# Key ring of five chunks, overlapping head groups, and row maxima turned by VectorE instead of TensorE

## The reference, cut to what matters

```
mod = (silu(c) @ wmod)                     # six vectors of 128
h = layernorm(x) * (1 + ca) + sa
q, k, v = h @ Wq + bq, h @ Wk + bk, h @ Wv + bv      # 16, 4 and 4 heads of 64
q, k = rotary(q), rotary(k)
logits = q . k / 8, masked causally;  w = softmax(logits);  out = (w . v) @ Wo + bo
x = x + ga * out
h = layernorm(x) * (1 + cb) + sb
x = x + gb * sum over the two best experts of weight * ((silu(h @ w1) * (h @ w3)) @ w2)
```

## Time and profile before

| | us |
|---|---|
| median of three runs | 1372.88 (1371.19 to 1373.23) |
| profiled execution, its own time | 1371.72 |
| its span, first to last instruction | 1369.8 |
| TensorE busy in the span | 1288.1 (94%) |
| VectorE busy | 916.7 (67%) |
| ScalarE busy | 566.6 (41%) |
| GpSimd busy | 551.8 (40%) |

### The profile page before, as it was taken

One profiled execution on the slowest core, in us unless ns is written; L12 is line 12 of the kernel. 1 busy time (PEld: TensorE's weight loads), 2 busy tenths in 40 slices (PEclk: granted clock), 3 DMA queues, 4 the chain that ended last, 5 costly groups with the idle time before them and its releaser, 6 DMA issues.

```text
span 1369.8 us, 18475 instructions
## 1 busy us (share of the span) xinstructions
PE 1288.1 (94%) x6732; PEld 808.2 (59%) x6732; DVE 916.7 (67%) x1775; ACT 566.6 (41%) x1178; POOL 551.8 (40%) x599
## 2 busy tenths in 40 slices
PE   2689999998999999899999999999995899999998
PEld 2445555455555555555555555555543688888887
DVE  3767877858687786868777687877648544444443
ACT  1444544554554355444444545444443222232222
POOL 2553446563354564446456344654422111110110
PEclk9799999999999999999999999999997899999999
DMA  5000000000000000000000000000001000000001
GB/s 134 1 0 1 1 1 1 1 1 1 1 1 1 1 1 1 1 1 1 1 1 1 1 1 0 1 1 0 1 1 47 0 24 23 23 23 23 23 1 31
DMA packets 18445, 12.94 MB, mean 9 GB/s; under 512 B 7104, under 2 KB 15680, under 8 KB 18368
## 3 DMA queue, kind: packets, MB, share of 16 engines
q1 hardware_dynamic: 11072, 9.58, 2.3%
q10 hardware_dynamic: 7296, 2.36, 0.7%
HBM read 10.88 MB, written 1.05 MB: 9 GB/s over the span
## 4 chain that ended last, share of the span: by engine, by line
PE 78%; DVE 14%; POOL 3%; issue 2%; ACT 1%; ACTq 1%; DVEq 0%; POOLq 0%
PE PS L1003 17%; PE PS L1051 13%; PE PS L957 10%; PE PS L985 10%; PE PS L1065 8%; PE PS L987 8%; DVE part_max L743 2%; PE PS L1013 2%; PE PS L934 2%; DVE full L759 2%; PE PS L1022 2%; PE PS L970 2%; PE PS L941 2%; DVE full L788 2%; DVE k_split L732 1%
## 5 line engine op out<-in xcount | busy, mean ns | idle before, releaser
L743 DVE TENSOR_REDUCE part_max<-PS 128x1 f32<-128x512 f32 (+2 forms) x576 | 348.0, 620 | 119.9 <-PE PS L957 94.5
L580 ACT ACTIVATE full<-PS 128x512 f32<-128x512 f32 x384 | 224.3, 598 | 230.0 <-PE PS L987 213.8
L957 PE MATMUL PS<-KT,QT 128*128 128x512 f32 (+3 forms) x640 | 262.8, 423 | 12.5 <-ACT QMT L562 5.0
L985 PE MATMUL PS<-QT,KT 128*128 128x512 f32 (+3 forms) x640 | 265.7, 415 | 1.0 <-ACT diag L589 1.0
L449 POOL TENSOR_TENSOR full<-full 128x512 f32<-128x512 f32 x128 | 165.6, 1320 | 176.8 <-PE PS L1003 175.7
L987 PE MATMUL PS<-QMT,KT 128*128 128x512 f32 (+3 forms) x640 | 233.7, 365 | 0.0
L957 PEld LDWEIGHTS PS<-KT,QT 128*128 128x128 f32 x640 | 120.7, 191 | 157.1 <-DVE part_max L743 86.9
L1003 PE MATMUL PS<-full,V 128*64 128x512 f32 x768 | 207.1, 618 | 0.0
L589 ACT ACTIVATE diag<-PS 128x512 f32<-128x512 f32 (+3 forms) x256 | 111.4, 438 | 227.8 <-PE PS L990 202.4
L853 DVE TENSOR_TENSOR full<-full,PS 128x512 f32<-128x512 f32 x128 | 88.0, 688 | 145.5 <-ACT full L629 145.5
L985 PEld LDWEIGHTS PS<-QT,KT 128*128 128x128 f32 x640 | 122.8, 192 | 90.8 <-ACT diag L589 32.1
(11 more groups left out here) (109 smaller groups left out, 1628.7 us busy)
## 6 DMA issues: line engine op xcount, KB each, us to landing
full<-in_L_ffn_experts_w_dram SPq DMA_DIRECT2D x24, 256.0 KB, 2.9
out_dram<-XA SPq DMA_DIRECT2D x4, 256.0 KB, 2.3
wqkv<-in_L_attn_Wq_dram ACTq DMA_DIRECT2D x1, 512.0 KB, 4.3
bqkv<-in_L_attn_bq_dram ACTq DMA_DIRECT2D x1, 512.0 KB, 10.1
wo_sb<-in_L_attn_Wo_dram SPq DMA_DIRECT2D x1, 512.0 KB, 8.7
sin_sb<-in_k_sin_dram ACTq DMA_DIRECT2D x1, 512.0 KB, 8.2
full<-in_L_wmod_dram SPq DMA_DIRECT2D x1, 384.0 KB, 9.5
cos_sb<-in_k_cos_dram ACTq DMA_DIRECT2D x1, 256.0 KB, 9.5
```

The costliest lines, as they stand in the source:

```text
L580: nc.scalar.activation(full[:, k % QUADS, r, :], PS[:, bank, :], ACT.Exp).then_inc(probs_ready, 1)
L743: nc.vector.reduce_max(part_max[:, t, b:b + 1], PS[:, bank, 0:width], AX.X).then_inc(ring_dve, 1)
L957: last = nc.tensor.matmul(PS[:, bank, 0:w], QT[:, ch % 2, h, t * P:(t + 1) * P], KT[:, 0, b * BANK:b * BANK + w], start=True, stop=not las ...
L985: nc.tensor.matmul(o, KT[:, 0, kt * P:(kt + 1) * P], QT[:, ch % 2, h, q0:BANK], start=True, stop=False)
```

## The change

`q_max` is gone. The negated maxima go to a small tile `neg_max` (128 queries x 4 heads x 4 tiles). In `maxed`, VectorE now issues four 32x32-block transposes, one for each 32 partitions, each reading one column for every tile broadcast 32 times and writing 32 partitions x 128 elements of a new tile `max_rows`; partition 64 of it is then the row of 512 maxima. Before them VectorE waits until ScalarE has copied the previous pair-step's row of the same m (`max_placed`). In `qmax`, TensorE and the ring have no part: ScalarE waits for the transposes and copies one row of 512 elements into row 64 of QMT. The 64 feature rows of QMT are written at `qk`, by one more ScalarE copy of 64 x 512 from the ring bank that holds the turned queries; ScalarE's copy into `q_max` at `low` is gone. QMT has two buffers, by chunk. TensorE waits at `s` for `max_placed` in place of the ring.

KT grows from four chunks to five (`KEY_SLOTS`), addressed as a ring over all groups' chunks by `key_at`, so the next group's first chunk has a place of its own. The groups' lists are merged by position, so that a group's last steps (its tail up to 9.3) lie between the first steps of the next. The placements of the next group's first steps and of the first maxima change.

```diff
@@ the order
-    begin.append(begin[-1] + 30.0)
+    begin += [begin[-1] + x for x in begin[1:3]]
-        place(maxima(2, 0), 0.05, 0.99),
-        place([("qmax", 2, 0)] + maxima(2, 1), 1.01, 1.74),
+        place(maxima(2, 0), 0.5, 1.25),
+        place([("qmax", 2, 0)] + maxima(2, 1), 1.27, 1.8),
-        place(parts(CHUNKS), 6.19, 7.16), place(turned(CHUNKS), 7.32, 7.47), place(max_steps(end), 7.4, 7.71),
-        place(parts(CHUNKS + 1), 7.42, 8.14), place(maxima(end + 1, 0) + maxima(end + 1, 1), 7.77, 7.85),
-        place([("qmax", end, 1)], 7.71, 7.79),
-        place(turned(CHUNKS + 1), 8.0, 8.36), place([("qmax", end + 1, m) for m in range(2)], 8.4, 8.7),
+        place(parts(CHUNKS), 5.1, 6.0), place(turned(CHUNKS), 6.1, 6.3), place(parts(CHUNKS + 1), 7.0, 7.8),
+        place(maxima(end, 0) + maxima(end, 1), 6.85, 7.4), place(maxima(end + 1, 0) + maxima(end + 1, 1), 7.4, 7.9),
+        place([("qmax", end, m) for m in range(2)], 7.9, 7.97),
+        place([("qmax", end + 1, m) for m in range(2)], 8.02, 8.3),
+        place(turned(CHUNKS + 1), 8.05, 8.5),
+        place(diag_steps(7), 8.03, 8.4), place(tail_steps(7), 8.45, 9.3),
+    steps += merge(*placed)
@@ tiles
-        q_max = sb("q_max", [P, 2, TB, QH, P], F32R)
+        neg_max = sb("neg_max", [P, QH, TB])
+        max_rows = sb("max_rows", [P, 2, BANK])
-        QMT = sb("QMT", [P, QH, BANK], F32R)
-        KT = sb("KT", [P, 2, T], F32R)
+        QMT = sb("QMT", [P, 2, QH, BANK], F32R)
+        KT = sb("KT", [P, 2, KEY_SLOTS * BANK], F32R)
+        def key_at(tile):
+            return tile // TB % KEY_SLOTS * BANK + tile % TB * P
@@ GpSimd
-            nc.gpsimd.memset(q_max[:, :, :, :, HEAD + 1:P].bitcast(F32), 0.0)
+            nc.gpsimd.memset(QMT[:].bitcast(F32), 0.0)
@@ ScalarE
-                nc.scalar.copy(q_max[:, ch % 2, b, :, 0:HEAD], q).then_inc(q_max_ready, 1)
+                        slot = n.slot_at[("q",) + x[1:]]
+                        act.wait_ge(ring_filled, slot + 1)
+                        src = PS[0:HEAD, RING + slot % RING_BANKS, :].rearrange("p (a b) -> p a b", a=QH)
+                        nc.scalar.activation(QMT[0:HEAD, ch % 2, :, t * P:(t + 1) * P], src, ACT.Copy)
-                        ring_to(QMT[:, 2 * (x[1] % PAIRS) + x[2], :], x, BANK)
+                        _, J, m = x
+                        act.wait_ge(max_ready, n.at["maxed", J, m] + 1)
+                        if J >= 2 * PAIRS:
+                            act.wait_ge(scores_ready, n.at["s", J - 2 * PAIRS, local(J - 2 * PAIRS), TB - 1, m] + 1)
+                        nc.scalar.copy(QMT[HEAD:HEAD + 1, J // PAIRS % 2, 2 * (J % PAIRS) + m, :],
+                                       max_rows[HEAD:HEAD + 1, m, :]).then_inc(max_placed, 1)
@@ VectorE, maxed
-                    dve.sem_inc(max_ready, 1)
+                    if J >= 1:
+                        dve.wait_ge(max_placed, n.at["qmax", J - 1, m] + 1)
+                    for a in range(P // 32):
+                        rows = slice(32 * a, 32 * (a + 1))
+                        to = max_rows[HEAD:HEAD + 32, m, :].rearrange("p (t q) -> p t q", q=P)[:, :, rows]
+                        last = nc.vector.transpose(to, neg_max[rows, 2 * (J % PAIRS) + m, :].unsqueeze(2)
+                                                   .broadcast_to([32, TB, 32]))
+                    last.then_inc(max_ready, 1)
@@ TensorE
-                elif kind == "qmax":
-                    _, J, m = x
-                    need(max_ready, n.at["maxed", J, m] + 1)
-                    bank = ring_bank(x)
-                    for t in range(TB):
-                        last = nc.tensor.transpose(PS[:, bank, t * P:(t + 1) * P],
-                                                   q_max[:, J // PAIRS % 2, t, 2 * (J % PAIRS) + m, :].bitcast(F32),
-                                                   ident[:])
-                    last.then_inc(ring_filled, 1)
-                    taken(("qmax", J, m))
+                    need(max_placed, n.at["qmax", J, m] + 1)
```

More of the change, by code:

```diff
@@ L166, in block_kernel @@
     next_group = [
-        place(parts(CHUNKS), 6.19, 7.16), place(turned(CHUNKS), 7.32, 7.47), place(max_steps(end), 7.4, 7.71),
-        place(parts(CHUNKS + 1), 7.42, 8.14), place(maxima(end + 1, 0) + maxima(end + 1, 1), 7.77, 7.85),
-        place([("qmax", end, 1)], 7.71, 7.79),
-        place(turned(CHUNKS + 1), 8.0, 8.36), place([("qmax", end + 1, m) for m in range(2)], 8.4, 8.7),
+        place(parts(CHUNKS), 5.1, 6.0), place(turned(CHUNKS), 6.1, 6.3), place(parts(CHUNKS + 1), 7.0, 7.8),
[4 more added lines that the diff above has]
+        place(diag_steps(7), 8.03, 8.4), place(tail_steps(7), 8.45, 9.3),
     ]
+    last_pair = [place(diag_steps(7), 8.01, 8.38), place(tail_steps(7), 8.4, 9.0)]
     def group_order(*more):
-        return merge([(float(b), x) for b, x in zip(before, main)], [(begin[end], x) for x in pending],
-                               *side, *more)
+        return [y for items in ([(float(b), x) for b, x in zip(before, main)], [(begin[end], x) for x in pending],
+                                *side, *more) for y in items]
     def of_group(order, g):
@@ L191, in block_kernel @@
             maxima_first = maxima_first[n:]
-    last_tail = place(tail_steps(-1), 0.02, 1.1)
     steps = of_group(lead_in, -1)
+    placed = []
     for g in range(GROUPS):
-        steps += of_group(group_order(*([last_tail] if g else []),
-                                      *(next_group if g < GROUPS - 1 else [place(tail_steps(end - 1), 8.4, 8.9)])), g)
+        order = group_order(*(next_group if g < GROUPS - 1 else last_pair))
+        at = [(p + g * begin[end], x) for (p, _), x in zip(order, of_group([x for _, x in order], g))]
+        placed.append(at)
+    steps += merge(*placed)
     class Counts:
@@ L213, in __init__ @@
                     "proj": [(x, "dve")], "qk": [(("q",) + x[1:], "act"), (("k",) + x[1:], "act")],
-                    "max": [(x, "dve")], "qmax": [(x, "act")], "rowsum": [(x, "dve")],
+                    "max": [(x, "dve")], "rowsum": [(x, "dve")],
                     "out": [(x, "dve")],
@@ L739, in step @@
                     if ch == 0:
[L740 removed]
+                        nc.vector.tensor_reduce(neg_max[:, 2 * (J % PAIRS) + m, t:t + 1],
                                                 PS[:, bank, 0:width], AX.X, ALU.max, negate=True).then_inc(ring_dve, 1)
@@ L956, in step @@
                     w = (t + 1) * P if last_bank else BANK
+                    keys = key_at(J // N_J * TILES + b * TB)
                     last = nc.tensor.matmul(PS[:, bank, 0:w], QT[:, ch % 2, h, t * P:(t + 1) * P],
-                                            KT[:, 0, b * BANK:b * BANK + w], start=True, stop=not last_bank)
+                                            KT[:, 0, keys:keys + w], start=True, stop=not last_bank)
                     if last_bank:
@@ L984, in step @@
                     o = PS[:, bank, q0:BANK]
-                    nc.tensor.matmul(o, KT[:, 0, kt * P:(kt + 1) * P], QT[:, ch % 2, h, q0:BANK],
+                    nc.tensor.matmul(o, KT[:, 0, keys:keys + P], QT[:, ch % 2, h, q0:BANK],
                                      start=True, stop=False)
-                    last = nc.tensor.matmul(o, KT[:, 1, kt * P:(kt + 1) * P], QMT[:, h, q0:BANK],
+                    last = nc.tensor.matmul(o, KT[:, 1, keys:keys + P], QMT[:, ch % 2, h, q0:BANK],
                                             start=False, stop=q < ch)
```

20 lines of the change are left out of this document (8 added, 12 removed).

## The result

The changed kernel takes 1390.12 us (median of four runs, 1388.83 to 1391.27) against 1372.17 us for the one before on the same chip (four runs, 1371.19 to 1373.23): a ratio of 1.0132, with a 95% interval of 1.0117 to 1.0146. Forecast were 1367 and a range of 1343 to 1386. The profiled execution took 1389.49 us, its span 1387.7.

The account below looks back on a forecast made before the run. TensorE was taken as the bound (94% busy), except some microseconds at group ends where VectorE leads. The sum was 1371.7 - 42.6 + 25 + 8.5 + 2 + 2 = 1366.6, given as 1367 us, range 1343 to 1386.

Parts of the forecast that it names:

- The new wait: At three group ends VectorE stands 9 to 10 us before maxed(9, 0); 8.3 us per end, 25 us in all.
- the same zero: Start of the walk through a group's end: where TensorE starts s(7,3,1,0), 303.16 in the old trace.
- the 4.8 chosen of two bounds: Eight quadsum adds on VectorE at a group's end, priced at 0.60 each; the other price kept was 0.86.
- Removed transposes of 26.2 us: TensorE's 64 times four transposes of the maxima, at 0.41 us for four, counted as 26.2 us saved.
- rival 3: TensorE's transposes stood where exponentials would hold it up anyway, so only part of 26 us is gained: about 1375; chance 0.08.
- VectorE's added work: 256 block transposes at 0.27 us, 1.1 per maxed, 70 us, mostly hidden; 8.5 us charged inside groups, bounds 0 and 20.
- the high bound: Upper price of a VectorE block transpose, 0.32 us (0.28 and a semaphore's gap); 0.27 was taken.
- the 3 us that the prediction gave it: Sum 3 us higher if VectorE's four transposes, starting in different 32-partition groups, are held and do not overlap.
- The lead-in, 2 us: First group's start: three or four maxed of 1.1 us in the chain, half hidden; 2 us, bounds 0 to 4.
- The order: Old waits of 4.5 us at each of three group ends, 13.5 us, removed since the order there is new.
- Rival 2: VectorE becomes the bound from 7.65 over the group's end to J = 3: +13.9, 1387 us; chance 0.20.
- its mark of 250: Group period of 250 us or more would show VectorE as the bound; the forecast had 245 to 247.

Follow-up runs that it names:

- the kernel with one transpose: Changed kernel with the row copy placed earlier, plus one 128-partition transpose and four ScalarE row copies per maxed in place of four transposes: 1370.47 us, ratio 0.9982.
- order alone: Kernel before the change with only the new order and five-chunk key ring, TensorE still turning the maxima: 1366.14 us (0.995), again 1367.28 us (0.9961).
- the earlier copy: Changed kernel with ScalarE's row copies at group ends moved from 7.9 to 7.42 in the order, ahead of VectorE's next maxed: 1376.77 us, ratio 1.003.

## Why the prediction was wrong, step by step

**The new wait: right.** The prediction named VectorE's stand before `maxed`(9, 0), what is queued behind it, and that TensorE would wait for the diagonal exponential. Foreseen and measured, from the same zero: the stand 9 to 10 us and 11.2; restart +2.5 and +2.4 (308.70 - 306.29); exponential +14.3 and +14.2 (320.52); TensorE at the step at +8.3 and +7.95 (321.17 - 6.93 - 306.29); idle 6.0 and 6.93. The quadsums took 4.89 us, as the 4.8 chosen of two bounds. Counted for a whole end were 8.3 us of idle; the waits of three ends in the profile, 21.3 for the exponential, 2.1 and 1.8, make 8.4 each.

**Removed transposes of 26.2 us: the step that failed.** They were counted in full, since TensorE was busy for all of 25 us. From one group's end to the next, before, after, and then a section of the kernel with one transpose (columns as in the earlier trace rows):

```profile
303.16:549.71 246.55, 240.78 (x1219) 131.97 (x1217) 188.68 (x344) 116.99 (x256) 126.31 (x137) 1.00 0.00 1
```
```profile
321.17:572.58 251.41, 239.01 (x1152) 126.86 (x1153) 200.44 (x410) 121.15 (x257) 124.51 (x136) 0.98 0.00 1
```
```profile
329.79:573.95 244.16, 236.54 (x1153) 124.96 (x1153) 189.72 (x360) 129.94 (x304) 125.27 (x137) 1.00 0.00 1
```

TensorE's idle time went from 5.8 to 12.4 us, close to what was forecast. But its busy time fell by 1.8 us in place of 6.6. Part of the missing 4.8 is the lower clock behind each stand: the work from 321.17 to 328.97 has 7.1 us of busy time, and 3.6 at the full clock (331.31 to 334.90 above). But in the third row the granted clock is 1.00 throughout, and the busy time is still only 4.2 below that of the kernel before; some 2.4 us have nothing to do with the clock, and no run says what they are. Three times 4.8, and the 4.5 by which the lead-in was missed, are 19 of the 23 us between forecast and result. The step fails without the standstill too: with one transpose VectorE is as busy as before the change (922 us), and against order alone the four sections differ by +1.5, -0.3, +1.0 and -3.3 us, 1.1 gained in all, where 26.2 were counted for the whole kernel. In the section of the third row the 4.1 us that did leave TensorE's busy time (240.7 with order alone) came back as idle time, 7.6 us in place of 3.8. In the stretch without a group's end, J = 24 to 31, the gain was 3.0 us (213.07 to 210.06) where 11 sets of transposes at 0.41, 4.5, were removed: a third of it was lost, and TensorE now waits for reduces and for QMT there. That is rival 3's statement, in part.

**VectorE's added work: mis-sized.** A `maxed` costs 1.25 us at 0.32 from start to start, the high bound; 1.1 was taken. By the Trainium skill ("VectorE: DVE Perf Modes", section "Two Vector instructions with no wait between them"), an instruction whose input starts in another group of 32 partitions than the last one's starts only when all earlier ones have finished. The traces agree: 0.32 apart with the change, 0.20 without. The price of the hold in this kernel is larger than the 3 us that the prediction gave it: without it the kernel, timed once, was some 11 us faster, in each of the four sections (-2.5, -2.1, -4.3, -1.8 between marks). That is with the standstill in place; without it, taking away far more of VectorE's time gave 6.3.

**The lead-in, 2 us: mis-sized.** It cost 6.5 to the first mark. Four `maxed` of 1.26 stand ahead of the first exponential, the last two in series with it and not half hidden; the exponential is 3.65 us late, and TensorE meanwhile is at the 1.2 GHz level until 80 us. With the first mark at 100.05 to 103.39 among kernels with the same lead-in, the split between chain and clock is not settled.

**The order: larger gain than given.** Without the new turning a group's period is shorter by 2.0 us (246.55 to 244.50), at each of three joins, 5 to 6 us in the kernel. All of it lies between the last mark of a group and the first of the next (16.97 to 15.06 us). The prediction let the new waits replace the old ones and gave the overlap no worth of its own.

**The sum by parts.** Order and ring -6, turning on VectorE +10.6 (7.5 of it in the lead-in by the profiles), the standstill +13.4 (1390.12 - 1376.77): +18. They are steps of one row of kernels, so that they add up says nothing by itself. Rival 2 came out nearest, 1387, and the period of 250.4 to 251.4 is past its mark of 250. That its sum is so close is in part luck: it had 11.5 us of idle time at an end (8.4 measured) and quadsums of 0.86 (0.61), and took off the full 26.2. Its place is narrower than was written: the stand itself, the lead-in, and the hold in each `maxed`. Open: what makes up the 1.5 us that turning costs in each section with a group's end though it takes 6.6 us off TensorE. The marks say where: some 3 us are lost between those of J = 6 and 7 (41.0 to 41.5 us with the earlier copy, 38.2 with order alone), and with one transpose they are still lost there (41.1 to 42.5), while TensorE's waits for reduces shrank from 7.2 us in 19 to 2.6 in 8. What is left at the three ends then is TensorE waiting for ScalarE, 5.5 us for the diagonal exponential and 5.2 for the copy to QT, waits that order alone doesn't have; no run takes them away. Transposing straight into QMT, with no row copy, was not tried.

## What to carry to other kernels

Where a staging tile has one buffer, look in the order for the place of its consumer's copy, not only of its producer: moving the copy half a pair-step earlier, or a second buffer, was worth 13 us, more than any other single part of the change. Work moved from the bound engine to one at 67% is not free: ask first for the form with the fewest instructions, since here one transpose did what four did. And time removed from an engine at the place where another leads for a moment comes back in part as idle time, so count it section by section.

## What the runs showed of the hardware

- A float32 block transpose takes 304 ns for 32x128, 310 for 128x128, and 712 for 128x512: the time goes with the free size, not with the partitions.
- Four of them with differing first partitions take 1.25 us, with one source 0.88.
- ScalarE's copy of a single row costs as much as one of 128 partitions: 615 ns for 512 elements (0.60 from PSUM in the earlier trace rows) and 295 for 128 (298 for a cast of 128 x 128).
- TensorE's granted clock fell from 1.00 to 0.50 within a stand of 6.9 us and stayed at 0.50 until 328 us, 7 us into the work behind it; with unread matmuls in the stand it was 1.00 to 326, and fell to 0.61 and 0.53 after the next short waits.
